# Hyperbolic attention in a two-block transformer kernel: the token turn a batch ahead, the projections and their copies earlier, the loop written out

## The reference

```python
q, k, v = (per_head(layernorm(x) @ w.T) for w in (wq, wk, wv))
diff_sq = q2 + k2 - 2.0 * qk                       # q2, k2: squared norms
denom = maximum((1.0 - q2) * (1.0 - k2), 1e-06)
dist = arccosh(maximum(1.0 + 2.0 * diff_sq / denom, 1.0))
out = softmax(-dist) @ v
x = x + out @ wo.T
```

## Time and profile before

| what | value |
|---|---|
| median of 3 runs | 2562.73 us (2561.97 to 2563.45) |
| profiled execution, its own time | 2565.39 us |
| span of the profiled execution | 2563.6 us |
| mean granted TensorE clock | 0.844 |
| busy share PE, DVE, ACT, POOL | 81%, 78%, 72%, 65% |
| hyperbolic attention | about 1300 to 2430 us of the span |

### The profile page before, as it was taken

One profiled execution on the slowest core, in us unless ns is written; L12 is line 12 of the kernel. 1 busy time (PEld: TensorE's weight loads), 2 busy tenths in 40 slices (PEclk: granted clock), 3 DMA queues, 4 the chain that ended last, 5 costly groups with the idle time before them and its releaser, 6 DMA issues. The chain is left out here.

```text
span 2563.6 us, 50172 instructions
## 1 busy us (share of the span) xinstructions
PE 2079.1 (81%) x14935; PEld 1515.9 (59%) x14935; DVE 1998.1 (78%) x6007; ACT 1854.7 (72%) x3188; POOL 1663.5 (65%) x1516
## 2 busy tenths in 40 slices
PE   4999999999999979999947666666666666666599
PEld 4777777777777668888834444443433444434266
DVE  4677777777777757877768999999999999999522
ACT  2666666666666634344239999999999999999743
POOL 2767766676667400000058999999999999999600
PEclk7999999999999969999966677777777777777599
DMA  5000000000000024334200000000000000000011
GB/s 136 1 2 2 1 1 0 1 0 1 1 0 1 2 67 108 93 92 110 68 1 1 1 1 0 0 0 0 0 0 0 0 0 0 0 0 1 7 31 37
DMA packets 44067, 49.03 MB, mean 19 GB/s; under 512 B 5112, under 2 KB 27038, under 8 KB 43934
## 3 DMA queue, kind: packets, MB, share of 16 engines
q1 hardware_dynamic: 35614, 43.32, 7.0%
q10 hardware_dynamic: 8320, 4.19, 0.7%
HBM read 42.78 MB, written 4.72 MB: 19 GB/s over the span
## 5 line engine op out<-in xcount | busy, mean ns | idle before, releaser
L1460 POOL TENSOR_TENSOR u<-u,spare 128x1024 f32<-128x1024 f32 x256 | 597.2, 2372 | 35.1 <-ACT spare L1433 34.9
L545 ACT ACTIVATE prob<-s_ps,nmax 128x128 f32<-128x128 f32 (+1 forms) x1024 | 364.4, 432 | 140.1 <-DVE nmax L602 140.0
L1353 PE MATMUL d_ps<-rowsT 28*128 28x256 f32 x1024 | 165.9, 404 | 331.3 <-DVE u L1532 331.2
L602 DVE CUSTOM_DVE_ANT_0 s_ps<-s_ps,mask 128x128 f32<-128x128 f32 (+1 forms) x1024 | 341.3, 385 | 101.8 <-issue 77.9
L1353 PEld LDWEIGHTS d_ps<-rowsT 28*128 28x128 f32 x1024 | 106.2, 242 | 430.4 <-issue 430.0
L582 POOL TENSOR_TENSOR g_lo<-g_all,g_hi 128x512 fp32r<-128x512 f32 x256 | 329.1, 1286 | 21.4
L1528 DVE TENSOR_SCALAR u<-d_ps 128x1024 f32<-128x1024 f32 x256 | 311.9, 1218 | 39.5 <-PE i_ps L1353 39.3
L1532 DVE SCALAR_TENSOR_TENSOR u<-i_ps,u 128x1024 f32<-128x1024 f32 x256 | 313.5, 1225 | 14.8
L1471 POOL TENSOR_TENSOR spare<-spare,u 128x1024 f32<-128x1024 f32 x128 | 303.1, 2368 | 10.7
L1447 ACT ACTIVATE u<-u 128x1024 f32<-128x1024 f32 x256 | 258.3, 1070 | 0.0
L1450 ACT ACTIVATE u<-u 128x1024 f32<-128x1024 f32 x256 | 257.5, 1066 | 0.0
(11 more groups left out here) (265 smaller groups left out, 5577.9 us busy)
## 6 DMA issues: line engine op xcount, KB each, us to landing
w_all<-w_rows SPq DMA_DIRECT2D x128, 256.0 KB, 5.6
x<-L_attn_x ACTq DMA_DIRECT2D x8, 512.0 KB, 14.0
y<-y_rows SPq DMA_DIRECT2D x16, 256.0 KB, 2.3
wkqv<-L_attn_Wkqv SPq DMA_DIRECT2D x4, 528.0 KB, 8.7
gate_rows<-L_ffn_gate_proj SPq DMA_DIRECT2D x1, 512.0 KB, 14.5
up_rows<-L_ffn_up_proj SPq DMA_DIRECT2D x1, 512.0 KB, 11.5
down_cols<-L_ffn_down_proj SPq DMA_DIRECT2D x1, 512.0 KB, 13.3
w_rows<-wT SPq DMA_DIRECT2D x8, 64.0 KB, 1.6
```

The source lines that it names most:

```text
L545: last = nc.scalar.activation(prob[:, kind, at, :].rearrange("p c n -> p (c n)"), s_ps[kind][:, at.start * P:at.stop * P], ACT.Exp, bias=n ...
L602: last = nc.vector.tensor_tensor_reduce(out=scores, in0=scores, in1=keep.mask[:, N - width:N], scale=-1.0, scalar=3.4e38, op0=ALU.add, op1 ...
L1353: last = nc.tensor.matmul(ps[:, e * W2 + j * N:e * W2 + (j + 1) * N], rowsT[at, slot(i, p), 1, j * P:(j + 1) * P], rowsT[at, slot(i, p), 0 ...
L1460: nc.gpsimd.tensor_tensor(u[:, slot(i, p), :], u[:, slot(i, p), :], spare[:, p % SPARE, :], ALU.add).then_inc(sum_done, 1)
```

## The change

Five edits, all in `hyperbolic_attention`:

1. PE turns the tokens of `b+2` at pair 7 of `body(b)`, not those of `b+1` at pair 0; ACT copies them (`act_xT`) after the square roots of pair 6, not after the table load. The output projection of `b-2` moves behind the turned rows of pair 7 and waits for that copy.
2. PE projects block 0 of `b+1` at pair 0 (before: 1) and block 1 at pair 1 (before: 2). ACT copies block 0 (`act_hi`) between the first two logarithms and the first two exponentials, not after the exponentials. DVE's `dve_lo` of block 0 moves from pair 2 to pair 1.
3. `dve_features_end` moves from pair 4 to pair 5, and the second `pe_turn_o` goes ahead of the last `pe_values` and the turn of row group 0.
4. POOL's `pool_product` loses its 4-element first instruction and the constant tile `twos`; the `tensor_scalar` takes all 1024 elements.
5. All 32 batches are written out, without registers and branches.

```diff
         def pe_turn_x(pe, b):
             pe.wait_ge(xh_done, (b + 1) * TB)
-            after(pe, res_done, b - 3)
+            after(pe, attnT_done, b - 3)
...
         def pe_qkv(pe, b, j):
             pe.wait_ge(xT_done, b + 1)
+            after(pe, res_done, b - 3)
...
-            nc.gpsimd.tensor_tensor(extra[:, 0:4], pair[:, 0:4], twos[:, :], ALU.add)
-            nc.gpsimd.tensor_scalar(extra[:, 4:2 * W2], pair[:, 4:2 * W2], 1.0, 2.0, ALU.mult, ALU.add).then_inc(raised, 1)
+            nc.gpsimd.tensor_scalar(extra, pair, 1.0, 2.0, ALU.mult, ALU.add).then_inc(raised, 1)
...
-        def over_batches(engine, body):
...
+        def over_batches(body):
+            for b in range(batches):
+                body(b, b % TURN, b >= 1, b >= 2, b >= 3, b + 1 < batches, b + 2 < batches)
...
-                        if one_after and p == 0:
-                            pe_turn_x(pe, b + 1)
-                        if one_after and p == 1:
-                            pe_qkv(pe, b + 1, 0)
+                        if b == 0 and p == 0:
+                            pe_turn_x(pe, 1)
                         for r in {0: (5, 6), 1: (7,)}.get(p, ()):
                             pe_turn_rows(pe, b, r)
+                        if one_after and p == 0:
+                            pe_qkv(pe, b + 1, 0)
+                        if two_before and p == BACK_AT + 1:
+                            pe_turn_o(pe, b - 2, 1, (i - 2) % TURN, b + 2 if one_after else batches)
                         if one_before and p in VALUES_AT:
                             pe_values(pe, b - 1, VALUES_AT.index(p), (i - 1) % TURN)
+                        if two_after and p == PROJECT_AT:
+                            pe_turn_x(pe, b + 2)
                         if one_after:
-                            if p == 2:
+                            if p == 1:
                                 pe_qkv(pe, b + 1, 1)
...
-                            if p == PROJECT_AT:
-                                pe_project(pe, b - 2)
...
+                        if two_before and p == PROJECT_AT:
+                            pe.wait_ge(xT_done, b + 3 if two_after else batches)
+                            pe_project(pe, b - 2)
...
-                def weights(b, i, p):
+                def weights(b, i, p, between=None):
                     for logarithm in (True, False):
                         for n in range(2):
                             act_weights(act, b, p + n, i, logarithm)
+                        if logarithm and between is not None:
+                            act_hi(act, between, 0)
...
+                        if two_after and p == 6:
+                            act_xT(act, b + 2)
...
                         if one_after:
-                            if p in (2, 4):
-                                dve_lo(dve, b + 1, p // 2 - 1, (i + 1) % TURN)
+                            if p in (1, 4):
+                                dve_lo(dve, b + 1, p // 4, (i + 1) % TURN)
                             if p == 4:
                                 dve_features(dve, b + 1)
+                            if p == 5:
                                 dve_features_end(dve, b + 1)
```

More of the change, by code:

```diff
@@ L1271, in hyperbolic_attention @@
         attnT = m.sb("attnT3", [P, N])
-        twos = m.sb("twos", [P, 4])
         part_stats = m.sb("part_stats3", [P, TB, 6])
@@ L1613, in body @@
                         if two_before:
-                            if BACK_AT <= p < BACK_AT + TB:
-                                pe_turn_o(pe, b - 2, p - BACK_AT, (i - 2) % TURN, b + 2 if one_after else batches)
+                            if p == BACK_AT:
+                                pe_turn_o(pe, b - 2, 0, (i - 2) % TURN, b + 2 if one_after else batches)
                             if p == ATTN_AT:
                                 pe_turn_attn(pe, b - 2)
-                            if p == PROJECT_AT:
-                                pe_project(pe, b - 2)
                         if one_after:
@@ L1622, in body @@
                                 pe_turn_rows(pe, b + 1, r)
-                over_batches(pe, body)
+                        if two_before and p == PROJECT_AT:
+                            pe.wait_ge(xT_done, b + 3 if two_after else batches)
+                            pe_project(pe, b - 2)
+                over_batches(body)
                 def finish(b):
@@ L1654, in body @@
                         nc.scalar.preload_act_table_set("natural_log_exp_and_others")
-                    if one_after:
-                        act_xT(act, b + 1)
+                    if b == 0:
+                        act_xT(act, 1)
                     for p in range(0, HP, 2):
                         if one_before:
-                            weights(b - 1, (i - 1) % TURN, p)
-                        if one_after and p in (0, 2):
-                            act_hi(act, b + 1, p // 2)
+                            weights(b - 1, (i - 1) % TURN, p, b + 1 if one_after and p == 0 else None)
+                        elif p == 0:
+                            act_hi(act, b + 1, 0)
+                        if one_after and p == 2:
+                            act_hi(act, b + 1, 1)
                         if two_after and p == 4:
@@ L1669, in body @@
                             copy_rows(act, b + 1, ROWS_BY_SCALAR[0], (i + 1) % TURN)
-                over_batches(act, body)
+                        if two_after and p == 6:
+                            act_xT(act, b + 2)
+                over_batches(body)
                 nc.scalar.preload_act_table_set("natural_log_exp_and_others")
@@ L1685, in _ @@
                 nc.gpsimd.memset(v[:, :, :, :, DH:VW], 1.0).then_inc(zeroed, 2)
-                nc.gpsimd.memset(twos[:, :], 2.0).then_inc(v_cleared, 1)
-                pool.wait_ge(v_cleared, 3)
                 def body(b, i, one_before, two_before, three_before, one_after, two_after):
@@ L1693, in body @@
                         pool_sum(pool, b, p, i)
-                over_batches(pool, body)
+                over_batches(body)
             @block.vector
@@ L1743, in body @@
                             dve_distances(dve, *following, i if p + 1 < HP else (i + 1) % TURN)
-                over_batches(dve, body)
+                over_batches(body)
                 dve_residual(dve, END - 2)
```

## The result

The changed kernel takes 2609.38 us (median of 4, 2602.03 to 2612.07), the one before 2563.09; the ratio is 1.0174 (1.0149 to 1.0198). It is slower by 46 us; 25 were forecast. The profiled execution took 2607.01 us. It runs from POOL's first memset of `rows` to ACT's `std_mlp`: 2431.39 - 1292.65 = 1138.7 us before, 2473.48 - 1286.14 = 1187.3 after. All of the loss is there.

What follows compares the result with a forecast made beforehand. The prediction took the loop through DVE and PE, with no engine full, as the bound. Its terms summed to +0.87 us a batch, over 29 batches +25 us, giving 2588 us; the forecast's range was 2572 to 2615.

Steps and rivals of the forecast that it cites:

- `dve_lo` for ACT: At block 0's earlier `dve_lo`, DVE newly waits for ACT's `sq`, behind row group 7's turn: +1.4 us a batch.
- behind pair 2: With `dve_lo` gone from pair 2, DVE waits there for the next pair products: +0.4 us a batch.
- behind pair 3: DVE's wait behind pair 3 may grow or shrink by 0.2 us: taken as 0.
- residual: Token turn moved into pair 7 delays the output projection, on which DVE's residual waits: +0.15 us a batch.
- features fill pair 5: `dve_features_end`, moved to pair 5, fills DVE's half us of wait there: -0.5 us a batch.
- second turned output: DVE's wait for the second turned output goes, as PE turns it earlier: -1.18 us a batch.
- pair 7: PE's early output turn waits for the first normalised output, delaying DVE's distances of pair 7: +0.75 us a batch.
- loop written out: Without the loop's turn, 0.15 us once in three batches, and the register waits: -0.15 us a batch.
- The rival in which ACT is the bound: Earlier copies give back ACT's wait of 0.8 us a batch, 2540 us; DVE's `dve_lo` wait under 0.5; chance 0.10.
- POOL's edit: Dropping the 0.20 us instruction, four a batch, is worth nothing on the path; 0.7 a batch if POOL were the bound.
- The signs: Expected waits: DVE at `dve_lo` 1.2 to 1.8 us, ACT at `act_hi` 1.5 or more, POOL about 2.5.
- The rival of a higher clock: PE's clock rises, halving PE's work in each new wait: 33.6 us a batch, 2545 to 2552 us; chance 0.20.

Runs made afterwards that it cites:

- experiment 1: Changed kernel with `dve_lo` of block 0 and the projection of block 1 back at pair 2: 2564.65 us, ratio 0.9996 to the kernel before.
- experiment 9: Kernel before with 16 transposes of the identity added in PE's gap ahead of pair 6: 2557.20 us, ratio 0.9905.
- experiment 11: Kernel before with one more DVE instruction in each batch, a memset of 128x512 at pair 0: 2586.33 us, ratio 1.0096.
- experiment 2: Changed kernel with two buffers for the feature rows, used in turn, so block 0's copy needn't wait for row group 7: 2568.18 us, ratio 0.9997.
- Experiment 4: Changed kernel with only the second output turn back behind the last values and row group 0: 2596.75 us, ratio 1.0016 to the kernel before.
- experiment 7: Kernel before with only the loop over the batches written out: 2569.85 us, ratio 1.0008.
- experiment 6: Changed kernel with `dve_lo` of block 0, block 1's projection and the second output turn in their old places: 2590.71 us, ratio 1.0003 to the kernel before.

## Why the prediction was right

The direction, the place of the main loss and the path came out as forecast; the size came out at half. Terms of the sum, us a batch, with DVE's waits in the changed kernel less those before:

| term | forecast | measured |
|---|---|---|
| `dve_lo` for ACT | +1.4 | +1.17 |
| behind pair 2 | +0.4 | +0.40 |
| behind pair 3 | 0 | +0.10 |
| residual | +0.15 | +0.38 |
| features fill pair 5 | -0.5 | -0.53 |
| second turned output | -1.18 | -1.18 |
| pair 7 | +0.75 | +0.90 |
| copy of the outputs | none | +0.29 |
| loop written out | -0.15 | not found |
| sum | +0.87 | +1.53 |

- **What bounds.** The period is DVE's work and its waits in the changed kernel (3.70, batch 35.6) and in experiment 1 (2.12, 34.1), but so it is for any engine; it doesn't show who sets the pace. Experiments 9 and 11 do: shorter pieces on PE shorten the batch, 0.485 us more on DVE lengthens it by 0.84. I put ACT 0.6 us under this loop; its wait in the earlier trace rows says 0.8.
- **`dve_lo`, +1.4.** Right in place and chain, shown by experiments 1 and 2; measured 1.17, the higher clock's value, in each batch. The rival in which ACT is the bound asked for less than 0.5 here and is out. Experiment 4 keeps this wait in full at a stage of 1144.6: the 1.18 saved at the turned output pays for it, and what loses is this wait together with that of pair 7.
- **Pair 7, +0.75.** I had weighed the higher clock in, and PE stood at the lower one (granted 0.50). The chain came to 1.07 in the batch shown, as worked out for the lower clock, and made DVE wait for `o_ps` as well, for which the sum has no term. Experiment 4 shows what hangs on this turn: 43 us of stage.
- **Residual, +0.15.** Too small; 9.1 / 24 = 0.38.
- **POOL and the written-out loop.** POOL's edit was hidden, as said. The loop's turn was misread: over 24 batches the intervals are mostly 34.17 to 34.21 where the loop turns and 34.11 elsewhere, so 0.08 once in three batches, not 0.15, and experiment 7 finds no gain at all.
- **The sum.** The mis-sized terms are pair 7 with the copy behind it (+0.44), the residual (+0.23), the loop (+0.15) and pair 3 (+0.10), against `dve_lo` (-0.23). By the table loads the batch grew by 35.61 - 34.14 = 1.47. The batch of 35.6 lies in the forecast's 34.4 to 36.5 and 2609 us in its 2572 to 2615, but 46 us is nearly twice the 25 of the sum: the middle was off, and the wide range covered it.
- **The signs.** ACT's wait at `act_hi` was to grow to 1.5 or more and grew from 0.80 to 1.11; beside it ACT now waits 0.93 for row group 0, which stands behind the early turn and which I hadn't foreseen. POOL's wait grew to 3.1, not 2.5.
- **The fallen clock** is not shown to be a cause of its own. In experiment 11 it fell by 0.07 and the batch grew by 0.84; in experiment 7 it fell by 0.07 and the batch grew by 0.11.
- **The rival of a higher clock** failed for the changed kernel; made true by hand in experiment 9 it pays. The Trainium skill (TensorE: Matmul & The Clock Gate, HAM oscillation) says that gaps cost clock each time they recur. This trace agrees: behind the gap the clock is 0.50 in the kernel before, and 1.00 in experiment 9, where the gap is filled in part.

Undoing the move of `dve_lo` or that of the turn alone recovers 48.5 or 43 us of 48.6, and both together no more. For each alone this adds up roughly: the change saves 1.71 (features and turned output), against which 1.67 of losses is left without the move and some 1.95 without the turn. With both undone 0.48 would be left and a batch would take 32.9, less than ACT's own 33.3; what came instead are the waits and the longer copy of experiment 6. Why it comes out at 34.15 again, and whether ACT, which waits 0.6 to 0.8 us a batch in each of these kernels and works the rest, sets that number, is open: no run changed ACT's work.

## What to carry to other kernels

Before moving a consumer earlier, follow its producer back to the engine that consumes: if the chain starts on that same engine, the work between start and consumer was its cover, here 4.26 us for a chain of 2.4. When a piece of work stands behind a gap of its engine, look at the granted clock of that stretch, not at the mean, and price the piece at the clock found there. Look also for a small instruction that has grown long: a copy of 128x4 took 1.44 us instead of 0.16 and was in no list of waits. And read the waits, not the busy shares: at 97.7% ACT still let an edit on PE shorten the batch, yet it is the limit once DVE's waits are short.

## What was not expected

Adding work made the kernel faster: 16 useless transposes in PE's longest gap, 2.02 us long in the batch shown, took 19.5 us off a stage of 1139. And a move of DVE's work that leaves POOL's list alone can still cost 1.28 us a batch, where it puts a tiny copy under a running POOL instruction.
